# Experts on tokens sorted by expert, in plain fp32, in a four-block network kernel on Trainium2

## The reference

```python
gates = softmax(x @ gW + gb)                      # 8 experts
top2_scores, top2_idx = top_k(gates, 2)
w = (one_hot(top2_idx, 8) * top2_scores[..., None]).sum(1)
h = relu(einsum('nd,edf->enf', x, W1) + b1[:, None, :])   # 256 -> 512
y = einsum('enf,efd->end', h, W2) + b2[:, None, :]        # 512 -> 256
out = einsum('ne,end->nd', w, y)
x = layernorm(x + out)
```

## Time and profile before

| | |
|---|---|
| median of 3 runs | 4840.15 us (4839.7 to 4841.41) |
| profiled execution, its own time | 4840.44 us |
| its span (first to last instruction) | 4838.7 us |
| mean granted TensorE clock | 0.865 of 2.4 GHz |
| PE busy | 3789.2 us (78%) |
| DVE busy | 3722.8 us (77%) |
| ACT busy | 2057.9 us (43%) |
| POOL busy | 1502.2 us (31%) |
| DMA queues | 16.3% and 0.6% of 16 engines' span |

### The profile page before, as it was taken

One profiled execution on the slowest core, in us unless ns is written; L12 is line 12 of the kernel. 1 busy time (PEld: TensorE's weight loads), 2 busy tenths in 40 slices (PEclk: granted clock), 3 DMA queues, 4 the chain that ended last, 5 costly groups with the idle time before them and its releaser, 6 DMA issues. The chain is left out here.

```text
span 4838.7 us, 64027 instructions
## 1 busy us (share of the span) xinstructions
PE 3789.2 (78%) x19288; PEld 1859.8 (38%) x19288; DVE 3722.8 (77%) x5114; ACT 2057.9 (43%) x2482; POOL 1502.2 (31%) x768
## 2 busy tenths in 40 slices
PE   4779999999999995799999637762666766646665
PEld 1413333233233325699999413320111111125554
DVE  5678888888888857554554696994898889878998
ACT  0426766666666671122222004561444344413332
POOL 0210000000000004000000131554888889844454
PEclk7969999999999997899999658885777777768887
DMA  1720110100101004200000222434111112121110
GB/s 60 238 67 4 38 37 6 38 17 24 39 3 39 3 5 136 70 18 9 9 9 0 67 98 79 145 115 128 59 56 55 54 55 64 55 66 46 43 35 13
DMA packets 214764, 254.44 MB, mean 53 GB/s; under 512 B 33992, under 2 KB 170064, under 8 KB 213328
## 3 DMA queue, kind: packets, MB, share of 16 engines
q1 hardware_dynamic: 208288, 242.29, 16.3%
q10 hardware_dynamic: 6320, 10.03, 0.6%
HBM read 142.30 MB, written 109.58 MB: 52 GB/s over the span
## 5 line engine op out<-in xcount | busy, mean ns | idle before, releaser
L856 DVE TENSOR_REDUCE att_maxima<-att_ps_m 128x1 f32<-128x512 f32 x2048 | 1281.0, 683 | 250.8 <-PE att_ps_m L899 247.1
L830 ACT ACTIVATE att_probs<-att_ps_s 128x1024 f32<-128x1024 f32 x1024 | 996.1, 1021 | 433.7 <-PE att_ps_s L913 431.0
L899 PE MATMUL att_ps_m<-att_ks,att_qs 96*128 (+1 forms) x2048 | 730.8, 393 | 46.8 <-DMA att_ks<-scratch_k 28.8
L913 PE MATMUL att_ps_s<-att_qs,att_ks 99*128 (+1 forms) x2048 | 612.9, 381 | 13.9 <-DMA att_qs<-att_m_parts 11.7
L2065 POOL TENSOR_TENSOR ss_ch<-ss_h,ss_c_rep 128x1024 f32<-128x1024 f32 x256 | 594.5, 2347 | 3.4 <-DVE ss_h L2111 3.2
L921 PE MATMUL att_ps_o<-att_probs,att_vs 128*32 128x512 f32 x4096 | 547.2, 606 | 0.4 <-ACT att_probs L830 0.4
L2086 ACT ACTIVATE ss_ps_d<-ss_ps_d,ss_a_neg 128x1024 f32<-128x1024 f32 x256 | 278.6, 1088 | 521.2 <-PE ss_ps_d L2151 521.0
L1274 ACT ACTIVATE ex_hid_whole<-ex_ps_h,ex_b 128x512 f32<-128x512 f32 x256 | 175.8, 689 | 561.8 <-PE ex_ps_h L1349 537.9
L899 PEld LDWEIGHTS att_ps_m<-att_ks,att_qs 96*128 (+1 forms) x2048 | 165.4, 97 | 641.5 <-DVE att_maxima L856 367.0
L2173 PE MATMUL ss_ps_y<-ss_ch,ss_sum_block 128*32 128x256 f32 x2048 | 211.7, 497 | 143.9 <-POOL ss_ch L2065 143.9
L2143 PE MATMUL ss_ps_x<-ss_stack,ss_spread 96*128 96x512 bf16 x512 | 196.5, 473 | 152.8 <-ACT ss_skip L2074 74.4
(11 more groups left out here) (369 smaller groups left out, 6634.0 us busy)
## 6 DMA issues: line engine op xcount, KB each, us to landing
scratch_steps<-si_parts SPq DMA_DIRECT2D x48, 512.0 KB, 6.1
ss_stack<-scratch_steps SPq DMA_DIRECT2D x256, 96.0 KB
att_qs<-scratch_q SPq DMA_DIRECT2D x192, 64.0 KB
scratch_v<-qkv_v_ext SPq DMA_DIRECT2D x8, 1024.0 KB, 4.4
att_vs<-scratch_v SPq DMA_DIRECT2D x8, 1024.0 KB
ex_w_whole<-in_W SPq DMA_DIRECT2D x16, 512.0 KB
scratch_xc<-si_xc SPq DMA_DIRECT2D x8, 1024.0 KB, 4.3
scratch_zs<-si_zs SPq DMA_DIRECT2D x8, 1024.0 KB, 4.3
```

Source lines behind the costliest of these rows:

```text
L830: act.activation(probs[:, (2 * kt + pair) % 4, :, :], ps_s[pair][:, :, :], ACT.Exp, scale=HD ** -0.5).then_inc(exp_done, 1)
L856: dve.tensor_reduce(maxima[:, j, c:c + 1], ps_m[BANK[j * QC + c]][:, :], AX.X, ALU.max).then_inc(maxed, 1)
L899: pe.matmul(ps_m[BANK[j * QC + c]][:, :], q, k, start=True, stop=True).then_inc(scored, 1)
L913: mm = pe.matmul(ps_s[pair][:, i, :], ks[0:ROWS, bass.ds(st // QC % 2, 1), h, kt * P:(kt + 1) * P], qs[0:ROWS, bass.ds(st // QC % 2, 1), b ...
```

## The change

The router's choice is used: each token's two kept pairs are written, as rows of xa, into a DRAM table sorted by expert, the experts run over tiles of that table, and the results are gathered back.

1. `attention_output` also ranks: for each group it counts on PE how many kept tokens of each expert come earlier (`count`), DVE makes from it each pair's row in the table (`find_places`), and POOL sends the rows there with indirect DMAs (`scatter`). At the end DVE makes a table of which expert and which rows each of the 72 tiles has, and SP writes 128 rows of zeros behind each expert's last row. xa stays in SBUF; the two stores of it are gone. All experts' weights are loaded whole at the start of this stage, on ACT's queue.
2. `experts` runs 72 tiles of 128 rows. The tile's expert and first row are read from the table into registers of PE, DVE and SP. Products are plain fp32; hidden rows have tokens in partitions, so they are turned on PE before the second product.
3. `moe_output` gathers the two results of each token with indirect DMAs on POOL, ACT scales them by their scores, and PE adds them to xa and gates x b2 in PSUM; DVE reads the sum there. `ps_b` has two buffers.
4. `head_attention` copies b1, in DRAM, into rows by expert, with one DMA on SP.
5. Several pipelines are written out in full (`unroll=True`) in place of the hardware loop.

The diff, cut to its core:

```diff
+REGION = T + P
+SORTED = T * 2 // P + E
...
 def head_attention:
                 load_quad(0, 0, True)
                 load_quad(1, 1)
+                    sp.dma_start(scratch.b1_rows.rearrange("o (e t p) -> p (o e) t", e=E, t=FT), scratch.io["b1"]).then_inc(b1_laid, 16)
                 store_shift(0)
...
 def attention_output:
+                for e in range(E):
+                    end = sp.value_load(route.ends[0:1, e:e + 1], min_val=e * REGION, max_val=e * REGION + T)
+                    sp.dma_start(scratch.sorted_x[bass.ds(end, P), :], heads[:, 0, 0, :]).then_inc(zeroed, 16)
...
+                def scatter(g, slot):
+                    pool.wait_ge(placed, g + 1)
+                    for t in range(g * GT, (g + 1) * GT):
+                        for a in range(2):
+                            pool.indirect_dma_start(scratch.sorted_x[:, :], bass.IndirectOffsetOnAxis(route.slots[:, a, t:t + 1], 0),
+                                                    xa[:, t, :], None).then_inc(scattered, 16)
+                run_stages(pool, GROUPS, (add_bias, 0), (gain_shift, 1), (scatter, 5), unroll=True)
+                pool.wait_ge(scattered, TILES * 2 * 16)
...
+                def find_places(g, slot):
+                    dve.wait_ge(counted, g + 1)
+                    c.then(dve.tensor_tensor(place[:, :, :], ps_c[:, 0:GT, :], over(ends[:, :].unsqueeze(1), [P, GT, E]), ALU.add))
+                    dve.tensor_tensor(ends[:, :], ends[:, :], ps_c[:, GT, :], ALU.add).then_inc(counts_taken, 1)
...
+                run_stages(dve, GROUPS, (find_places, 5), (shift_logits, 4), (add_src, 1), (take_best, 4), (normalise, 1), unroll=True)
...
+                for e in range(E):
+                    act.dma_start(route.w1[:, e, :, :], io["W1"][e:e + 1, :, :].rearrange("o (k p) f -> p (o k) f", p=P)).then_inc(w_loaded, 16)
+                    act.dma_start(route.w2[:, e, :, :], io["W2"][e:e + 1, :, :].rearrange("o (k p) c -> p (o k) c", p=P)).then_inc(w_loaded, 16)
...
 def experts:
+                def load_x(m, slot):
+                    row = sp.value_load(route.table[0:1, 1, bass.ds(m, 1)], min_val=0, max_val=E * REGION - P)
+                    if third_on(m):
+                        sp.wait_ge(x_turned, m - 1)
+                    sp.dma_start(x[:, slot, :], scratch.sorted_x[bass.ds(row, P), :]).then_inc(x_loaded[slot], 16)
+                    if isinstance(m, int) and m == 1:
+                        sp.dma_start(b1[:, :], over(scratch.b1_rows, [P, E * FF])).then_inc(b_loaded, 16)
+                def store_y(m, slot):
+                    sp.wait_ge(y_taken, m + 3)
+                    sp.dma_start(scratch.sorted_y[bass.ds(m * P, P), :], y[:, slot, :]).then_inc(y_stored[slot], 16)
+                run_stages(sp, SORTED, (load_x, -2), (store_y, 3))
...
+                run_stages(act, SORTED, (take_y, 3))
...
+                dve.wait_ge(b_loaded, 16)
+                def add_b1(m, slot):
+                    e = dve.value_load(route.table[0:1, 0, bass.ds(m, 1)], min_val=0, max_val=E - 1)
+                    dve.wait_ge(h_ready, m + 3)
+                    dve.wait_ge(h_turned, m + 1)
+                    dve.tensor_tensor(hid[:, slot, :], ps_h[slot][:, :], b1[:, bass.ds(e * FF, FF)], ALU.add).then_inc(h_biased, 1)
...
+                run_stages(dve, SORTED, (copy_x, 0), (add_b1, 1), (clip_hidden, 2))
...
+                def expert_of(m):
+                    return pe.value_load(route.table[0:1, 0, bass.ds(m, 1)], min_val=0, max_val=E - 1)
+                def turn_x(m, slot):
+                    pe.wait_ge(x_loaded[slot], (m // 2 + 1) * 16)
+                    pe.wait_ge(x_split, m + 1)
...
+                def hidden(m, slot):
+                    e = expert_of(m)
+                    pe.wait_ge(x_split, m + 3)
+                    pe.wait_ge(h_biased, m + 1)
+                    for k in range(KC):
+                        mm = pe.matmul(ps_h[slot][:, :], x_t[:, slot, k, :], w1[:, bass.ds(e, 1), k, :].rearrange("p a f -> p (a f)"),
+                                       start=k == 0, stop=k == KC - 1)
...
+                def turn_hidden(m, slot):
+                    pe.wait_ge(h_biased, m + 3)
+                    pe.wait_ge(h_split, m + 1)
...
+                def output(m, slot):
+                    e = expert_of(m)
+                    pe.wait_ge(h_split, m + 3)
+                    pe.wait_ge(y_taken, m + 1)
+                    for f in range(FT):
+                        mm = pe.matmul(ps_y[slot][:, 0, :], hid_t[:, slot, f, :], w2[:, bass.ds(e, 1), f, :].rearrange("p a c -> p (a c)"),
+                                       start=f == 0, stop=f == FT - 1)
+                run_stages(pe, SORTED, (turn_x, 0), (hidden, 1), (turn_hidden, 2), (output, 3))
...
 def moe_output:
+                def gather(g, slot):
+                    if third_on(g):
+                        pool.wait_ge(bias_ready, g - 1)
+                    for a in range(2):
+                        for t in range(GT):
+                            pool.indirect_dma_start(back[:, slot, a, t, :], None, scratch.sorted_y[:, :],
+                                                    bass.IndirectOffsetOnAxis(route.packed[:, a, g * GT + t:g * GT + t + 1], 0)).then_inc(gathered[slot], 16)
+                run_stages(pool, GROUPS, (gather, -2), (scale_y, 0), (scale_xn, 3), unroll=True)
...
+                def weigh(g, slot):
+                    act.wait_ge(gathered[slot], (g // 2 + 1) * 2 * GT * 16)
...
+                run_stages(act, GROUPS, (copy_gate_t, -1), (weigh, -1), (all_rstd, 0, STEPS), (copy_xn, 4), unroll=True)
...
                     for t in range(GT):
+                        pe.matmul(ps_b[slot][:, t, :], gate_t[:, t * P:(t + 1) * P], b2[:, :], start=True, stop=False)
+                        pe.matmul(ps_b[slot][:, t, :], ident[:, :], route.xa[:, g * GT + t, :], start=False, stop=False)
+                        for a in range(2):
+                            mm = pe.matmul(ps_b[slot][:, t, :], ident[:, :], back[:, slot, a, t, :], start=False, stop=a == 1)
```

More of the change, by code:

```diff
@@ L148, in run_stages @@
     first, last = max(starts) + max(starts) % 2, min(ends) - min(ends) % 2
+    if unroll:
+        for s in range(min(starts), max(ends)):
+            step(s, s % 2)
+        return
     for s in range(min(starts), first):
@@ L1330, in _ @@
[L1330 to L1337 removed]
+                dve.sem_inc(x_split, 2)
+                dve.sem_inc(h_biased, 2)
+                dve.sem_inc(h_split, 2)
```

437 lines of the change are left out of this document (222 added, 215 removed).

## The result

The changed kernel takes 4516.05 us (median of 4 runs, 4511.07 to 4527.52) against 4839.92 for the kernel before (4 runs beside it, 4834.04 to 4841.41): a ratio of 0.9336, 95% interval 0.9316 to 0.9356. The forecast was 4571, 269 less than before; the gain is 324. Its profiled execution took 4513.32 us, with a span of 4511.6.

What follows compares the result with a forecast made beforehand. No one engine bounds the whole; TensorE alone set the experts' end, and PE's sequencer would after the change. 4840.4 - 357 (experts) + 50 (`attention_output`) + 28 (`moe_output`) + 10 (attention) = 4571 us, range 4480 to 4740.

Steps and rivals of the forecast that it cites:

- the sequencer's: Experts: PE's instruction issue, with two register reads at 1.0 us, takes 4.9 us a tile and sets it, rounded to 5.0.
- 75 full steps: Experts: the pipeline over the 72 tiles has 75 steps, each priced at 5.0 us.
- rival 1: Experts: register reads are free and the array binds at 4.2 us a tile, 4510 to 4490 in all; chance 0.17.
- Weight loads: Start of `attention_output`: 8 MB on ACT's queue make the first heads and src land some 7 us later.
- Scatters: `attention_output`: 64 indirect DMAs on POOL at 1.2 us each, 76.8 us.
- Waits of POOL inside steps 5 to 8: `attention_output`: a term of 1 us in the sum for POOL's end.
- sum from 1881: `attention_output`: 1881 + 7 + 1 + 102.6 + 3 for landing = 1995, against 1946, so +50 us.
- the DVE term: `attention_output`: DVE's added routing steps, at 0.2 us each, cost 2 us a group.
- The 10: Attention: the DMA turning b1 into rows delays the first store of the shift, +10 us.
- Draining reads: Experts: register reads empty PE's queue, 6.3 us a tile, +98 us, 4669 in all; chance 0.15.
- Dear indirect DMAs: `attention_output` and `moe_output`: 2.34 us for each indirect DMA issue on POOL, 4692 in all; chance 0.14.
- Half clock in the experts: Experts: PE never gets the high clock, array times double, 4.2 to 8.4 us a tile; 4984 with draining reads; chance 0.05.

Runs made afterwards that it cites:

- w_late: The changed kernel with the 16 weight loads issued two behind each group's copy of heads, none at the start of `attention_output`: 4507.78 us.
- b1_later: The changed kernel with the DMA that lays b1 out in rows issued in `attention_output` behind the loads, not in the attention: 4515.97 us.
- noreads: The changed kernel with PE's two register reads per tile left out, every tile multiplied by expert 0's weights: 4513.6 us.
- lag4: The changed kernel with everything from the turn of xa to the scatter one step nearer, scatters four steps behind in place of five: 4523.18 us.
- pe_bias: The changed kernel with POOL's add_bias in `attention_output` taken away and the bias added by PE in PSUM: 4535.05 us.
- reads3: The changed kernel with each of PE's two register reads per tile made three times: 4633.57 us, one run.
- scatter96: The changed kernel with 96 scatters in place of 64, each tile's first copy also sent to a spare tensor: 4559.42 us, one run.

## Why the prediction was right or wrong

**What bounds.** Right: PE's array set the experts' stretch and still does, with PE busy 298 of 311 us at a clock of 0.98.

**Experts, the tile.** The term that failed is the sequencer's: "2 x 1.0 + 2.0 + 0.9 = 4.9 against 4.2 for the array", and so 5.0. I took the price of a read from "nearer to the DMA since it too crosses to memory and back", and it is 0.30 us by its record and 0.65 with its steps. The rest of the sum was too high as well: the sequencer needs 3.2 to 3.3 a tile, which leaves some 2.0 (an estimate) for what had been put at 2.9. So the array's 4.2, which had come from the earlier trace rows, is what a tile takes: 4.08. 75 x 0.92 is 69 of the 80 us; 9 more are in counting 75 full steps, where the three that fill and empty the pipeline are short (296.7 us from the first hidden product to the last copy on ACT). Start (10.2 us, forecast 11) and tail (3, forecast 4) were right. This was rival 1, with 0.17; on the rows it deserved more, since the array's price was read and the sequencer's guessed. The Trainium skill's floor for a tensor_load ("DMA: Bandwidth & Descriptors", Latency and other measured facts), some 600 ns, lies above the record of 303 ns and near the 0.65 us of a read with its steps; by it too the array would have been the bound.

**attention_output.** Four terms were short, 28 us in all. Weight loads: forecast 7, measured 13.6, since "ACT's own issues, 16 x 0.4, lie inside that wait" is false; they block (`w_late`). Scatters: 1.27 in place of 1.2, 4.5 us. Waits of POOL inside steps 5 to 8: forecast 1, measured 13.1 (10.2, 0.9, 1.2 and 0.8 ahead of the last four `gain_shift`). And from the end of the last scatter it is 8.6 us to the first x load, where I had 3 for the landing: its rows have landed at 2027.6, and then POOL's drain at the end of the block takes 5.28 us in the trace.

The larger part of the wait ahead of the fifth `gain_shift` was there to be read. Here it is in the kernel before and in after (timeline):

```profile
1890.24 2.34 POOL L1077 TENSOR_TENSOR ao_y<-ao_y,ao_gain 128x1024 f32<-128x1024 f32 x1 [6.79 <-DVE ao_y L132]
```

```profile
1917.79 2.36 POOL L1131 TENSOR_TENSOR ao_y<-ao_y,ao_gain 128x1024 f32<-128x1024 f32 x1 [10.19 <-DVE ao_y L132]
```

6.8 of the 10.2 us are the idle time of the kernel before. The prediction took it as filled by scatters, and its sum from 1881 has no term for it; but the first eight scatters stand behind this `gain_shift` in POOL's program. The other 3.4 fit the DVE term, though no run isolates it: "2 us a group" was reckoned at 0.2 an operation, a price of rows where POOL was idle. In after some of the new operations, and one of them beside scatters, are (timeline):

```profile
1970.56 0.19 DVE L1215 TENSOR_TENSOR ao_place<-ao_ps_c,ao_ends 128x32 f32<-128x32 f32 x1
1970.61 2.34 POOL L1131 TENSOR_TENSOR ao_y<-ao_y,ao_gain 128x1024 f32<-128x1024 f32 x1 [0.84 <-DVE ao_y L132]
1970.79 0.16 DVE L1217 TENSOR_TENSOR ao_ends<-ao_ends,ao_ps_c 128x8 f32<-128x8 f32 x1
1970.87 2.16 DVE L1218 TENSOR_TENSOR ao_picked<-moe_chosen,ao_place 128x64 f32<-128x64 bf16 x1
...
1973.32 2.08 DVE L1222 CAST moe_slots<-moe_places 128x8 int32<-128x8 f32 x1
...
1980.56 0.22 DVE L1218 TENSOR_TENSOR ao_picked<-moe_chosen,ao_place 128x64 f32<-128x64 bf16 x1
1980.72 0.96 POOL L1139 DMA_INDIRECT scratch_sorted_x<-moe_xa,moe_slots  x1 [0.31 <-issue]
```

L1218 is 0.22 us alone or beside a scatter, and 2.16 beside a POOL pass of 2.34: it waits until the pass is over. L1222, a cast from one tile in SBUF, waits out the next pass. That is the earlier trace rows's 1.38 turned to 5.67 in another place, and I had not carried it over. The Trainium skill ("SBUF — State Buffer", SBUF: two separate sides) tells of a port pair shared by the two engines that one of them holds for a whole instruction; the trace agrees for L1218, which reads two tiles in SBUF, and L1217, which reads PSUM and SBUF and lies inside the same pass, is not touched at 0.16.

**moe_output.** Right, +27.3 for +28, and its parts nearly so: DVE's first read of PE's sum 36.3 us behind the start in place of 18.1 (forecast +22, measured +18, as the products took 14.3 and not 17), the seven steps behind them 151.9 in place of 142.1 (+9.8; forecast +12 less 6), steady step 24.0. Two errors of 4 us cancel, so the closeness of the sum is luck. A gather is 0.95 us and 1.25 from the next. Not forecast and hidden in the sum: POOL's drain at the end is 7.7 us in place of 2.4, and POOL stood 6.9 us waiting for constants that its gathers don't need.

**Attention.** Right, +10.5 for +10, and `b1_later` shows the cause. The mean price of a packet times the elements had given 15.6; the measured 10.5 is some 41 ns an element over 16 engines. The 10 was a value chosen between that 15.6 and nothing, so the hit owes something to luck; and with the same code ahead of it, `attention_output` starts at 1823.4 to 1827.9 in the traces, so the stage's figure is good to some 2 us.

**Rivals.** Draining reads: out (`noreads`). Dear indirect DMAs: out, 0.96 us at the median, and so too with DVE's small operations beside them. But the hold-up that this rival spoke of exists. Three of the 64 gathers of after took 1.7 us, and each started inside a DVE add of two tiles in SBUF (L1605), here DVE's row and POOL's:

```profile
2483.59 1.23 DVE L1605 TENSOR_TENSOR mo_x<-mo_v,mo_x 128x1024 f32<-128x1024 f32 x1
```

```profile
2483.95 1.69 POOL L1638 DMA_INDIRECT mo_back<-scratch_sorted_y,moe_packed  x1 [0.30 <-issue]
```

That is 2.2 us in the whole stage, far from the rival's price. Half clock in the experts: out, 0.98. Plain products in the old layout confirmed the prices of the earlier trace rows to 6%, so the array side of the sum was sound.

**The range and the sum.** 4480 to 4740 held 4516, by rival 1 on one side (-80) and a stage dearer than its bound of forecast on the other (+28). The two misses are of opposite sign, so that the total is off by 55 us and not by 80 is luck: the prediction had the wrong bound for the experts, which its rival 1 had right.

## What to carry to other kernels

Price each instruction queue and the array apart, and where one side's price is read from rows and the other's guessed, let the forecast lean on the read one. A DMA issue is not a constant: behind several large loads on one queue it blocks, so what stands behind it in program order (here the first copy of the stage) is late. Where a stage is a loop of hand-overs between engines, take what an edit adds to one turn of the loop, not to the busiest engine's total: drawing work forward (`lag4`) or off the busiest engine (`pe_bias`) gained nothing or lost.

## What the runs showed of the hardware that I had not expected

- A register read from SBUF is 0.30 us on PE, 0.31 on DVE and 0.27 on SP (TENSOR_LOAD rows), and 0.65 us of PE's queue with its steps (`reads3`). PE's sequencer takes it ahead of the array's work.
- An indirect DMA of 128 rows of 1 KB is 0.96 us of POOL, one each 1.27 us. Gathers that started inside a DVE add of two SBUF tiles (1.22 us) took up to 1.7 us in after. A block in which POOL issued them ends with a drain of POOL of 5.28 us (`attention_output`) and 7.68 us (`moe_output`, 2.44 before).
- ACT's issues of 512 KB loads went from 0.48 to 4.30 us once six were out.
- DVE operations of 0.2 us waited out POOL passes of 2.34 us, but only some: L1217, with one operand in PSUM, did not (0.16).
- With one weight row (`pe_bias`) a plain fp32 product of 256 columns has the same two records as one with 128.
- Open: up to 19.1 us at a stretch in which DVE waited for counts that PE had started long before, in two kernels (`b1_later`, `w_late`), and such waits of up to 28.6 and 9.7 us in two more (`scatter96`, `lag4`) of the twelve kernels with scatters.
